# Second attention: two tiles of distances ahead of the projection and of the values of tile three

## The reference

```
P = (Xn @ W_in.T + b_in)            # per head: Q, K, V, G
sq = q2 + k2 - 2 * Q @ K.T          # squared distances
W = (1e-4 + sqrt(max(sq, 0))) ** -2
W = W / (1e-4 + sum(W))
O = G * (W @ V)
X + O @ W_out.T + b_out
```

## Time and profile before

| | |
|---|---|
| time of three runs | 3915.79 us median (3913.46 to 3922.16) |
| time of the profiled execution | 3922.57 us |
| its span | 3920.8 us |
| granted TensorE clock, mean over the span | 0.941 |
| busy share of the span | PE 90%, DVE 64%, ACT 57%, POOL 16% |

### The profile page before, as it was taken

The page is one execution under the profiler, slowest core; times in us unless marked ns, Lnnn a source line. Parts: engine busy times, 40 slices in busy tenths (PEclk is TensorE's granted clock), DMA queues, the critical chain, the costliest instruction groups (busy, mean ns, idle before and its releaser), DMA issues.

```text
span 3920.8 us, 56053 instructions
## 1 busy us (share of the span) xinstructions
PE 3543.4 (90%) x22244; PEld 2491.0 (64%) x22244; DVE 2494.0 (64%) x4347; ACT 2228.7 (57%) x2875; POOL 646.5 (16%) x595
## 2 busy tenths in 40 slices
PE   4999999989999999978779779779877999999998
PEld 3555555478888899973323323323326888889998
DVE  4777777553433455547988988988985443335554
ACT  1666666643322344438998998998993332234443
POOL 3333332100122011221300300200000002200212
PEclk7999999899999999988889889889888999999999
DMA  3000000010011134430000000000001001013342
GB/s 123 1 1 1 1 1 1 1 65 6 25 37 32 34 94 115 105 76 8 1 1 1 1 1 1 1 1 1 1 1 65 6 22 38 24 45 91 94 111 40
DMA packets 86664, 124.81 MB, mean 32 GB/s; under 512 B 7752, under 2 KB 73115, under 8 KB 86402
## 3 DMA queue, kind: packets, MB, share of 16 engines
q1 hardware_dynamic: 68738, 100.05, 7.5%
q0 software_dynamic: 17664, 21.17, 3.3%
HBM read 85.02 MB, written 42.55 MB: 33 GB/s over the span
## 4 chain that ended last, share of the span: by engine, by line
PE 32%; ACT 10%; DVE 9%; issue 3%; DVEq 1%; ACTq 0%; POOL 0%; DMA 0%; SPq 0%; POOLq 0%
PE f2ring L1479 14%; PE f2acc L1498 7%; DVE b_w L1831 6%; ACT b_w L1869 5%; PE b_acc L1946 4%; PE b_ring L1958 4%; ACT b_w L1909 4%; ACT L1906 1%; PE b_ring L2008 1%; DVEq L1770 0%; PE b_ring L2006 0%; DVE b_stacks L1747 0%; PE b_ring L1982 0%; PE f2ring L1444 0%; DVE b_w L1775 0%
## 5 line engine op out<-in xcount | busy, mean ns | idle before, releaser
L1831 DVE TENSOR_TENSOR b_w<-b_w 128x2048 f32<-128x2048 f32 x254 | 571.7, 2292 | 25.7 <-ACT b_w L1909 21.7
L1869 ACT ACTIVATE b_w<-b_ring 128x1024 f32<-128x1024 f32 x512 | 485.9, 1037 | 92.2 <-PE b_ring L1958 86.3
L1946 PE MATMUL b_acc<-b_w,b_vg 128*32 128x512 f32 x2048 | 333.0, 740 | 172.6 <-DVE b_w L1831 171.5
L1909 ACT ACTIVATE b_w<-b_w 128x2048 f32<-128x2048 f32 x256 | 468.7, 1897 | 2.1 <-issue 0.4
L1399 ACT ACTIVATE f2hid<-f2ring 128x512 f32<-128x512 f32 (+2 forms) x256 | 132.6, 518 | 577.4 <-PE f2ring L1479 560.4
L1399 ACT ACTIVATE f1hid<-f1ring 128x512 f32<-128x512 f32 (+2 forms) x256 | 132.6, 518 | 576.8 <-PE f1ring L1479 559.8
L1317 DVE TENSOR_TENSOR f1hid<-f1hid,f1ring 128x512 f32<-128x512 f32 (+2 forms) x256 | 150.2, 587 | 439.4 <-ACT f1hid L1399 439.4
L1317 DVE TENSOR_TENSOR f2hid<-f2hid,f2ring 128x512 f32<-128x512 f32 (+2 forms) x256 | 150.2, 587 | 439.3 <-ACT f2hid L1399 439.2
L1958 PE MATMUL b_ring<-b_qT,b_kT 32*128 32x512 f32 x2048 | 411.4, 692 | 18.6 <-ACT b_w L1869 15.0
L1775 DVE TENSOR_SCALAR b_w<-b_w 128x2048 f32<-128x2048 f32 x256 | 305.7, 1225 | 86.7 <-ACT b_w L1869 85.8
L624 ACT ACTIVATE a_prob<-a_wide 128x1024 f32<-128x1024 f32 (+1 forms) x320 | 292.8, 943 | 86.5 <-PE a_wide L730 59.6
(11 more groups left out here) (340 smaller groups left out, 6274.9 us busy)
## 6 DMA issues: line engine op xcount, KB each, us to landing
X<-expert_in SPq DMA_DIRECT2D x16, 650.0 KB, 4.8
expert_in<-a_zeros SPq DMA_DIRECT2D x8, 650.0 KB, 10.1
X<-in_x SPq DMA_DIRECT2D x4, 1024.0 KB, 10.7
x_mid<-X SPq DMA_DIRECT2D x8, 512.0 KB, 3.1
f1raw_x<-in_rd SPq DMA_DIRECT2D x4, 1024.0 KB, 5.3
f1raw_xf<-in_rg SPq DMA_DIRECT2D x4, 1024.0 KB, 5.0
f1raw_xf<-in_ru SPq DMA_DIRECT2D x4, 1024.0 KB, 7.1
f1raw_g<-in_rg SPq DMA_DIRECT2D x4, 1024.0 KB, 4.9
```

Source lines behind the costliest of these rows:

```text
L1831: v.tensor_tensor(one(m), one(m), one(m), ALU.mult).then_inc(s_wts, 1)
L1869: s.activation(w[:, m, 2 * pair:2 * pair + 2, :].rearrange("p h n -> p (h n)"), slot(at + pair), ACT.Ln, scale=SHEP_EPS ** -2).then_inc(R. ...
L1909: s.activation(one(m), one(m), ACT.Sigmoid, scale=-0.5).then_inc(s_sig, 1)
L1946: last = pe.matmul(acc[32 * h:32 * h + 32, qc, :], vg[:, u % 2, h, x, :], w[:, x, h, :], start=(x == 0), stop=(x == TB - 1))
```

## The change

In a period's order, the first two tiles of distances of the next period now both stand ahead of the values of tile 3. The moved steps that are left by then stand between the two. A `project` is no longer placed among the values of tiles 0 to 2 but always in that place, behind the first tile of distances. The other tiles of distances stand one ahead of each of the values of tiles 4 to 7, and two behind them.

```
--- before.py
+++ after.py
@@ -1552,15 +1552,14 @@
         aux = aux[2:]
         for m in range(TB):
             if m == TB - 5:
-                out += aux + ahead[:1]
-                aux = []
-            elif m > TB - 4:
-                out += ahead[m - TB + 4:m - TB + 5]
-            elif m < TB - 5:
+                out += ahead[:1] + aux + ahead[1:2]
+            elif m > TB - 5:
+                out += ahead[m - 2:m - 1]
+            elif aux and aux[0][0] != "project":
                 out += aux[:1]
                 aux = aux[1:]
             out += [("values", j, m)]
-        return out + ahead[4:]
+        return out + ahead[6:]
```

## The result

The version after takes 3961.47 us (median of four runs, 3954.42 to 3966.82) against 3916.45 us before. The ratio is 1.0112, with a 95% interval of 1.0091 to 1.0133: it is 45 us slower by the medians, and the forecast of no difference with its range of 3900 to 3934 us was wrong.

The account below looks back on a forecast made before the run. ACT's waits for distances (85.1 us before the logarithms) were taken to bound the kernel; -2.5 + 1 + 2 - 3 + 1.5 = -1 us gave 3921.6 us against the profiled execution, 3915 us on the median's scale, range 3900 to 3934 us.

Parts of the forecast that it names:

- The order of steps: Changes from sigmoids to logarithms without a projection: waits only move, 1.57 us in 22 of 25; sum 45.6 instead of 48 us.
- The clock: PE's gap ahead of the second tile's second pair: the clock falls after one in seven even periods, +2 us.
- the held pair: Second pair of the second tile of distances: waits until the first logarithm frees a ring slot, 0.59 us for ACT.
- The three stretches behind `tokens`: Logarithms after a period with `tokens`: everything at twice the time, two more turns, 3.2 becomes 3.7 us each.
- The late start behind the moments: Three periods whose predecessor computed moments: values of tile 2 and first distances come late, +0.3 us each, 1 us.
- the low-clock price of 3.7 us: An ordinary stretch whose clock falls in the gap: waits 3.7 us instead of 1.57.
- The projections: `project` behind the first distances: -1 us in each of three first periods, +0.5 in each of three second ones.
- the second rival's case: Projections at the full clock, lifted by distances and values in front: -16.5 instead of -1.5 us, 3900 us; chance 0.23.
- The bound on the other side: First-period projection at the lower level all along: twice 6.3 us, ending at 2109, +5 us each.
- Its wait of 13 us: ACT's wait in a first period if the projection runs at the lower level all along, against 8.0 us before.
- the third: Clock falls in the new gap: 2.1 us each in half of 19 ordinary periods, +20 us, 3935 us; chance 0.17.
- The bound of 40 us: Upper bound of the clock's cost in ordinary periods: 19 x 2.1 us.

Follow-up runs that it names:

- The run with 128 rows: Version after plus overwritten full-row matmuls, two each ahead of the values of tiles 1 and 2 and the second tile of distances: 3924.89 us, 1.0018 of before.
- the one with 32 rows: Version after plus extra matmuls in those same places, each using 32 rows of the array instead of 128: 4055.13 us, 1.0358 of before.
- the run with full rows: Version after plus 128-row matmuls ahead of the values of tiles 1 and 2 only, none ahead of the second tile: 3947.61 us, 1.0080 of before.
- the run with the value between: Version after, but the values of tile 3 stand between the first and second tiles of distances: 3928.64 us, 1.0030 of before.

## Why the prediction was wrong

- **The order of steps** was read rightly. Where the clock is up, one wait of 0.59 and then 0.13 and 0.36 in turn, 1.57 us, is what the version after shows, to the hundredth, and what 19 stretches show with the clock kept up.
- **The clock is the step that failed.** The term was 2 us: a fall in the gap between the early and the held pair, in one of seven stretches after even periods, and nothing after odd ones because the gap there is short ("values 2 and distances ... last up to it"). Measured, 15 of the 22 ordinary stretches ran with the clock down, at 4.5 us on average instead of 1.57, which is 44 us. The forecast's mechanism, a clock that is up and falls in the new rest, holds in three of the fifteen. In the other twelve the clock was down already and did not come up, nine of them without any rest in front of the held pair. The forecast asked only what could bring the clock down. It did not ask whether the pairs that now run alone would let it rise as values 3 and 4 had. The run with 128 rows gave 37 us back and the one with 32 rows none, and behind `tokens` the pairs run together brought the clock up 3.5 us earlier. The rule of the Trainium skill that was weighed ("TensorE: Matmul & The Clock Gate", section on HAM oscillation) had the sign right. Its picture, a wait that sends the clock down, is what the rest of 2.20 us shows in three stretches and the rest of 2.29 us in the run with full rows.
- **The smaller terms.** The three stretches behind `tokens` were put at 3.7 us and wait 4.5 to 4.6. The late start behind the moments was put at 0.3 us each and is 0.7.
- **The price of a pair** is a second omission: the pairs of the second tile were known to be apart, but the low-clock price of 3.7 us did not count that the early pair alone then costs a whole tile's time; it pushes the fourth tile back as well (0.82 us in the first stretch above). The earlier trace rows had the number, four matmuls in 2.08 us against eight in 2.09. The Trainium skill ("TensorE: Matmul & The Clock Gate", section on the mechanism of row tiles) says that matmuls on different row groups run at once; the trace agrees, since a tile's two pairs together take the 2.1 us of one.
- **The projections** were forecast at -3 us in first and +1.5 us in second periods. They gave -12.7 and -2.3 us of wait (8.0 to 3.8 us and 4.3 to 3.6 us, three each): the second rival's case, at -15.0 us where it had -16.5. The term took the projection at 10.54 us, and it took 6.64. The bound on the other side, the whole projection at the lower level, was real too; it came in the run with the value between, with the same steps ahead of it. Its wait of 13 us is not what the text works out (a projection that ends at 2109 gives 9.1 us and 1.2 for the rest), but it is near the 11.2 to 12.3 us measured there.
- **The rival that came true** for the ordinary stretches is the third, slower by the clock, but with its reason, a fall in the gap, in three of fifteen only. Its size of 2.1 us a stretch was too small (2.9) and its share of one half too low. The bound of 40 us stood in the text and was taken for an extreme. Together with the gain of the projections, 47 - 15 us of wait and 6 us of lost overlap make 38 of the 39 us of the profiled periods. The whole span grew by 36 us; the profiled execution of before was 6 us above its median and that of after 3 us below its own, which makes the 45 us.

Open: why the clock rose just ahead of the logarithms in three stretches of the version after and not in nine others with the same steps ahead of them, and just ahead of the projection in one order and not in the other.

## What to carry to other kernels

When work is moved on TensorE, ask of each stretch not only whether the engine is busy but with what, and at which granted clock the row stands; two rows of equal busy time can be a factor of two apart. A tile that is made of groups that run at once should start when all of them can run: half a tile early cost here as much time as the whole, and resting instead was 25 us faster. The same steps at the same distances led to waits of 1.57 and 4.7 us, and of 3.8 and 12.2 us, by where the clock rose, so an order is judged by all its stretches and not by one. Where an edit has two parts, time them apart: one of these gave -0.2% and the other +1.9%.

## What the runs showed of the hardware

- The clock stayed at its lower level, granted 0.50, over 20.00 us in which PE was busy without a break, when the extra matmuls used 32 rows; with 128 rows in the same places it was 0.93 over 20 us around another change to logarithms.
- A projection that began at the lower level stayed there to its end: 12.5 us at 0.50 with TensorE busy throughout, against 6.64 us at 1.00 for the same instructions.
- Out of a rest of some 7 us at 0.50, the clock was up 3.5 us after the second tile began with its pairs together, and 7.1 us after its held pair began alone.
- The clock fell just behind a rest of 2.29 us, and in six stretches of the same run it held through rests of 1.2 to 1.4 us. In another run it held once through a rest of 2.27 us and fell at others as long.
- A pair of distances on half the rows takes 1.1 us at the full clock and 2.0 us at the lower, the same as the whole tile on all rows.
